# Eight of the last tile's projections computed in the attention stage, from operands read back from DRAM, and the layer norm's scaling moved from VectorE to ScalarE

## What is computed

```python
xn = layernorm(x)                      # x: (4, 1024, 512), no scale, no shift
q, k, v = xn @ Wq.T, xn @ Wk.T, xn @ Wv.T          # 16 heads of 32
scores = q @ k.T / sqrt(32), causal;   probs = softmax(scores)
attn = (probs @ v) @ Wo.T
gate = silu((xn @ fp8(gate_w)) * gate_scale)       # inner width 1536
up = (xn @ fp8(up_w)) * up_scale
ffn = ((gate * up) @ fp8(down_w)) * down_scale
out = x + attn + ffn
```

## Time and profile before

| what | value |
|---|---|
| runs | 1288.33, 1288.65, 1291.38 us, median 1288.65 |
| profiled execution, first to last instruction | 1287.4 us |
| PE busy | 1230.8 us, 96% |
| DVE, ACT, POOL busy | 1036.1, 895.2, 873.5 us |
| first stage | to 287.6 us |
| an iteration without and with output projections | 59.2 to 62.1, 59.7 us |
| transfers | 196 MB, mean 152 GB/s |

### The profile page before, as it was taken

The page is one execution under the profiler, slowest core; times in us unless marked ns, Lnnn a source line. Parts: engine busy times, 40 slices in busy tenths (PEclk is TensorE's granted clock), DMA queues, the critical chain, the costliest instruction groups (busy, mean ns, idle before and its releaser), DMA issues.

```text
span 1287.4 us, 32439 instructions
## 1 busy us (share of the span) xinstructions
PE 1230.8 (96%) x11756; PEld 822.8 (64%) x11756; DVE 1036.1 (80%) x2615; ACT 895.2 (70%) x1527; POOL 873.5 (68%) x1017
## 2 busy tenths in 40 slices
PE   4999999997999999999999999999999999999988
PEld 3444444445766767676777677777767677777663
DVE  8888887877877888788878788888888888878762
ACT  4322323228878888788888788888878888888770
POOL 1333232107877787788888888978878788888882
PEclk9999999998999999999999999999999999999999
DMA  8599998855645475666667676767686766767655
GB/s 271 161 250 243 256 258 232 203 152 120 135 96 129 96 151 99 145 114 148 127 138 153 127 153 125 157 104 166 115 158 114 160 121 137 143 128 165 105 113 121
DMA packets 427599, 196.07 MB, mean 152 GB/s; under 512 B 339248, under 2 KB 396592, under 8 KB 427440
## 3 DMA queue, kind: packets, MB, share of 16 engines
q1 hardware_dynamic: 409024, 177.22, 63.2%
q10 hardware_dynamic: 18416, 16.78, 4.9%
HBM read 72.89 MB, written 42.21 MB: 89 GB/s over the span
## 4 chain that ended last, share of the span: by engine, by line
PE 40%; POOL 16%; ACT 8%; issue 6%; DVE 5%; DMA 2%; SPq 0%; ACTq 0%; POOLq 0%; DVEq 0%
PE bank L1519 12%; PE bank L1533 12%; POOL row L1216 7%; PE bank L1495 6%; PE pair L210 3%; PE pair L1457 3%; POOL fuse L1198 3%; POOL probs L1064 3%; ACT probs L1263 3%; PE pair L1471 2%; POOL p L1210 2%; DMA p_t<-row 2%; ACT row L1287 2%; PE pair L1541 2%; DVE row_top L1399 2%
## 5 line engine op out<-in xcount | busy, mean ns | idle before, releaser
L1273 ACT ACTIVATE p<-pair,s_exp 128x512 f32<-128x512 f32 (+1 forms) x384 | 243.4, 634 | 143.3 <-PE pair L1457 142.0
L1216 POOL TENSOR_TENSOR row<-row 128x896 f16<-128x896 f32 (+1 forms) x128 | 256.2, 2011 | 7.7 <-ACT row L1287 7.7
L1263 ACT CAST probs<-p 128x512 f16<-128x512 f32 (+1 forms) x384 | 214.9, 560 | 15.1 <-POOL p L1210 12.6
L1064 POOL TENSOR_TENSOR probs<-p,probs 128x512 f16<-128x512 f32 x192 | 221.1, 1155 | 0.2
L1519 PE MATMUL bank<-shared,wu 128*128 128x256 f16 x1536 | 202.7, 276 | 0.0
L1519 PE MATMUL bank<-shared,wg 128*128 128x256 f16 x1536 | 202.5, 275 | 0.0
L1533 PE MATMUL bank<-wd,fuse 128*128 128x512 f16 x768 | 191.7, 380 | 0.8 <-DVE ff_out L1380 0.8
L1399 DVE TENSOR_REDUCE row_top<-pair 128x1 f32<-128x896 f32 (+1 forms) x128 | 147.5, 1152 | 35.4 <-PE pair L1475 34.9
L1210 POOL TENSOR_SCALAR_AFFINE_SELECT p<-p 128x128 f32<-128x128 f32 (+1 forms) x256 | 109.6, 433 | 93.2 <-ACT p L1273 91.3
L1198 POOL TENSOR_TENSOR fuse<-fu,fuse 128x512 f16<-128x512 f32 x96 | 118.5, 1235 | 65.3 <-ACT fuse L1302 65.1
L1519 PEld LDWEIGHTS bank<-shared,wg 128*128 128x128 f16 x1536 | 143.2, 98 | 25.0 <-DMA shared<-xn_parts 0.8
(11 more groups left out here) (155 smaller groups left out, 2106.0 us busy)
## 6 DMA issues: line engine op xcount, KB each, us to landing
q_st<-q_parts SPq DMA_DIRECT2D x192, 64.0 KB, 2.3
k_st<-k_parts SPq DMA_DIRECT2D x192, 64.0 KB, 2.0
v_parts<-res SPq DMA_DIRECT2D x8, 1056.0 KB, 6.8
v_sb<-v_parts SPq DMA_DIRECT2D x64, 132.0 KB, 2.2
xn_parts<-x_t SPq DMA_DIRECT2D x16, 512.0 KB, 8.8
q_parts<-qk_st SPq DMA_DIRECT2D x32, 256.0 KB, 5.5
k_parts<-qk_st SPq DMA_DIRECT2D x32, 256.0 KB, 4.2
shared<-xn_parts SPq DMA_DIRECT2D x16, 512.0 KB, 4.9
```

The lines of the kernel that those rows point to most:

```text
L1064: ops.tensor_tensor(probs[n % 2][:, LO, at], p32[e % RING][:, 0:UNIT_WIDTH[u]], probs[n % 2][:, HI, at], ALU.subtract).then_inc(signal, 1)
L1216: nc.gpsimd.tensor_tensor(row16[r][:, w:2 * w], row32[r][:, :], row16[r][:, 0:w], ALU.subtract).then_inc(row_lo, 1)
L1263: nc.scalar.copy(probs[n % 2][:, HI, u * 512:u * 512 + w], p32[e % RING][:, 0:w]).then_inc(p_hi, 1)
L1273: nc.scalar.activation(p32[e % RING][:, 0:w], st_bank[u % 2][:, 0:w], ACT.Exp, scale=s_exp[:, :]).then_inc(exp_done, 1)
```

## The change

Three things are done together.

1. Of the last tile (t = 7, `LAST`) only the four v projections stay in the first stage (`chunks`). In tile 6 the order is q, v, k (`chunk`). SP also stores the turned Wq and Wk to DRAM (`keep_weights`, 1 MB each, behind projections 7 and 8 of tile 6). In the second stage ACT loads the last tile's turned x (two halves of 0.5 MB) and Wq ahead of its first exponential, and Wk in head 1 of iteration 0. The eight q and k projections are made in the bank and at the steps of the output projections, in (iteration, head) (0, 1), (0, 2), (0, 3), (1, 2), (1, 3), (2, 2), (2, 3) and (3, 2), each in three pieces of 8 matmuls of 256 columns. ACT copies the HI part and DVE subtracts the LO part at step 4, SP stores it between the two turns of the rows, and PE waits for the LO part before the next turn of the maxima.
2. The normalisation of tiles 1 to 7 is made by ACT, as four activations (scale 1/sigma, shift -mean/sigma, both from POOL, which has two more links and a wait), behind projection 0 (6 in tile 0) and with `x_high` one projection later.
3. The plan of the feed-forward parts is denser: 4 parts in tiles 1, 2 and 6 and the last in tile 7; the row maxima of heads 0 and 1 move from tiles 6 and 7 to 5 and 6; the turn of head 0's maxima stands behind projection 1 of tile 6 and not 0.

```diff
+FF_STEPS = {2: ((1, 1), (1, 2), (1, 3)), 3: ((1, 3), (1, 4), (1, 5)), 4: ((1, 6), (1, 7), (1, 8)),
...
+            19: ((6, 0), (6, 1), (6, 1)), 20: ((6, 2), (6, 3), (6, 4)), 21: ((6, 5), (6, 6), (6, 7)),
+            22: ((6, 8), (6, 9), (6, 10)),
+            23: ((7, 9), (7, 10), (7, 11))}
+MAXIMA_AT, SPREAD_AT, FACTORS_AT = (6, 11), (7, 8), (7, 9)
+WEIGHTS_KEPT = {(6, 7): 0, (6, 8): 1}
...
+NORMALISED = (6, 0)
+LAST = NT - 1
...
+DEFERRED_AT = {(0, 1): 0, (0, 2): 1, (0, 3): 2, (1, 2): 3, (1, 3): 4, (2, 2): 5, (2, 3): 6, (3, 2): 7}
+DEF_STEP = {1: 0, 2: 1, 3: 2}
+DEF_SPLIT_STEP = 4
...
+        def chunks(t):
+            return range(12) if t < LAST else range(8, 12)
...
+        def chunk(t, c):
+
+            return (c, c + 4, c - 4)[c // 4] if t == LAST - 1 else c
...
+            def keep_weights(m):
+                sp.wait_ge(wt_act, 2 * (m + 1))
+                sp.wait_ge(wt_dve, 2 * (m + 1))
+                sp.dma_start(keep["w_dram"][m:m + 1].rearrange("a p w k d -> p (a w k) d"),
+                             w_t[m][:, :, :, :].rearrange("p w k d -> p (w k) d")).then_inc(w_stored, 16)
...
+            def normalise(t):
+
+                wait(act, xhi_done, t)
+                wait(act, xlo_done, t)
+                act.wait_ge(factor_link, FACTOR_LINKS * (t + 1))
+                for i in range(NB):
+                    last = nc.scalar.activation(xn[:, i, :], x_in[:, i, :], ACT.Identity, bias=shift[:, i:i + 1],
+                                                scale=rstd[:, i:i + 1])
+                last.then_inc(xn_done, 1)
...
-                    if c == (7 if t == 0 else 2) and has_next(t):
+                    if c == NORMALISED[t > 0] and has_next(t):
+                        normalise(t + 1)
+                    if c == NORMALISED[t > 0] + 1 and has_next(t):
                         x_high(t + 1)
...
-            last_tile = {0: ("magnitude 21", "add 21"), 1: ("off 21",), 2: ("magnitude 22",), 3: ("add 22",),
-                         4: ("off 22", "maxima"), 5: ("magnitude 23", "add 23"), 6: ("off 23",), 9: ("factors",)}
...
-                        if head == 1 and c == 0:
+                        if head == 1 and c == 1:
                             turn_maxima(nc, pe, rows, bank[7], ident, 0)
...
+            for half in range(2):
+                act.dma_start(late_x[half].rearrange("p w k t -> p (w k) t"),
+                              xn_dram[ds(NIT - 2 + half, 1)].rearrange("a p w k t -> p (a w k) t")
+                              ).then_inc(late_x_loaded[half], 16)
+            load_deferred_weights(0)
...
+            def high_of_deferred(d):
+                act.wait_ge(def_mm, d + 1)
+
+                wait(act, def_stored[d % 2], 16 * (d // 2))
+                nc.scalar.copy(def_st[d % 2][:, HI, :], misc[:, :]).then_inc(def_hi, 1)
...
+            def project_deferred(d, piece):
+
+                if piece == 0:
+                    pe.wait_ge(late_w_loaded[d // 4], 16)
+                    for half in range(2):
+                        pe.wait_ge(late_x_loaded[half], 16)
+                terms = [(wp, xp, kc) for wp, xp in X_TERMS for kc in range(KC)]
+                products = [(half, m) for half in range(2) for m in range(len(terms))]
+                for half, m in products[piece * 8:piece * 8 + 8]:
+                    wp, xp, kc = terms[m]
+                    mm = nc.tensor.matmul(misc[:, half * FT:(half + 1) * FT],
+                                          late_w[d // 4][:, wp, kc, d % 4 * P:(d % 4 + 1) * P],
+                                          late_x[half][:, xp, kc, :], start=(m == 0), stop=(m == len(terms) - 1))
...
+                            elif (it, s) in DEFERRED_AT:
+                                pe.wait_ge(def_lo, DEFERRED_AT[it, s] + 1)
```

More of the change, by code:

```diff
@@ L421, in tile @@
                                  ).then_inc(xt_stored, 16)
-                for c in range(8):
+                for c in chunks(t):
                     if (t, c) in HEADS_LOADED:
@@ new lines, in plan_of @@
+            def plan_of(t):
+                if t == 0:
+                    return first_tile
+                others = {(2, 11): ("max 3",), (3, 5): ("power 3",), (4, 11): ("low 3",),
+                          MAXIMA_AT: ("maxima",), FACTORS_AT: ("factors",)}
+                plan = part_steps(t)
+                for c in range(12):
+                    plan[c] = plan.get(c, ()) + others.get((t, c), ())
+                if t + 2 < NT:
+                    c = 9 if t + 2 == LAST else 10
+                    plan[c] = (f"statistics {t + 2}",) + plan[c]
+                return plan
```

199 lines of the change are left out of this document (129 added, 70 removed), and 6 rows, old and new, of the table FF_STEPS.

## The result

The changed kernel takes 1294.17 us (median of 4 runs, 1293.30 to 1295.46), the kernel before 1288.8 in the same runs: the ratio is 1.0040, 95% interval 1.0028 to 1.0053. Run once more later, beside an experiment, it took 1291.56 us, ratio 1.0018 (0.9999 to 1.0036). So it is slower by some 0.2 to 0.4% (the second time not clear of no change), and 21 to 23 us above the forecast of 1271. Its profiled execution spans 1291.6 us.

The account below looks back on a forecast made before the run. PE was taken to bound the first stage; the second had rests to fill. Terms -21.4 + 2.0 + 2.4 + 0.5 + 0.5 + 0.5 - 2.3 = -17.8 us took the 1287.4 span to 1269.6, plus 1.25: 1271 us, range 1265.5 to 1279.

Parts of the forecast that it names:

- Part 2: First stage, each tile: ACT normalises instead of DVE, covered by 3 us of slack; price 0, between 0 and 1 us per tile.
- Rival E: First stage, projections 1 and 2 of seven tiles: ACT's queue holds PE in each tile; 1292 us, chance 0.04.
- Part 1: First stage: eight projections leave, 20.7 us of PE, plus 0.65 us of waiting for POOL; gain 21.4 us.
- Part 3: Tile 6, denser DVE plan: PE waits behind projection 2 for the copied row of maxima, 2.0 us (0 to 3).
- Part 4: End of first stage: DVE's last "off" ends later, 2.4 us (1 to 4), plus 0.5 for the clock (0 to 1.7).
- Part 5: Start of second stage: ACT's three load issues cost 0.5 us (0 to 1.1), late operands 0.5 (0 to 2.4).
- rival B: Transfers bind: the first stage's stores only just fit and operands come 2.4 us late; 1275.5 us, chance 0.15.
- Part 6: Iterations 0 to 3 of the second stage: deferred projections fill PE's rests and lift its clock; -2.3 us (-5 to +5).

Follow-up runs that it names:

- e13: The changed kernel with DVE normalising tiles 1 to 7 again and POOL's two extra links gone: 1274.69 us.
- e2: The changed kernel with the up-weight loads of parts 13 and 16 issued at projection 8 of tiles 3 and 4, behind both x transposes: 1282.35 us.
- e1: The kernel before with only ACT's normalisation of tiles 1 to 7 and POOL's two extra links added: 1292.99 us, ratio 1.0044.
- e11: e8 with DVE normalising tiles 1 to 7 again, without POOL's two links or the edit on tile 0's wait: 1268.52 us.
- e3: The changed kernel with all twelve projections kept in tile 7, none deferred, and no late loads: 1308.08 us.
- e5: The changed kernel with ACT's first three late loads issued behind its second exponential of iteration 0: 1291.90 us.
- e6: The changed kernel with SP storing the fourth head's deferred projection (iterations 0 to 2) behind the row's second transpose: 1289.60 us.
- e8: e7 plus the edits of e5 and e6, and tile 0's normalisation not waiting for POOL's two new links: 1273.91 us.
- e7: The changed kernel with the edits of e2 and e4 together: 1276.29 us.
- e9: The changed kernel with the up-weight loads of parts 13 and 16 set to projection 5 of tiles 3 and 4, one later: 1290.56 us.
- e14: e11 with 14 instead of 7 matmuls keeping PE busy behind its last projection: 1268.60 us.
- e4: The changed kernel with DVE copying head 0's row of maxima ahead of its plan step behind projection 1 of tile 6: 1287.39 us.
- e15: The changed kernel with the up-weight loads of parts 13 and 16 set to projection 6 of tiles 3 and 4: 1288.89 us.
- e16: The changed kernel with ACT normalising tiles 2 to 7 behind its copy of projection 1 instead of 0: 1277.01 us.
- e19: e16 plus four edits of e8: row copy first, late loads later, store behind the row's transpose, tile 0 without the link wait: 1271.21 us.
- e10: e8 with 14 instead of 7 matmuls keeping PE busy behind its last projection: 1273.76 us.
- e12: e10 with DVE taking the row maxima ahead of its plan steps in tiles 5 and 6: 1273.55 us.

## Why the prediction was wrong

**The step that failed is Part 2**, "Price 0, between 0 and 1 us per tile". Undone, that one part gives 1274.69 (e13): inside the predicted range, 3.7 us above the forecast. All the rest was worth 14.6 us of the 17.8 forecast. Part 2 cost 17 to 20, of which the collision of one load and two transposes is the larger share (10.7 us in the profiles, tiles 3 and 4; moving the load alone, e2, brings the second stage 10.9 us forward). Three things were wrong in it.

First, it measured ACT's lateness by one user alone, PE's banks. There the slack of 3 us was nearly right: PE waits once at projection 5, the sign that was named for E, for 0.61 us in tile 2. It also saw that DVE would idle 3 us more and set that against DVE's spare time. But the same copies release DVE's low parts, these SP's stores, and SP's transposes are queued behind them. Second, it took the factors as ready 5.6 us behind the tile's start and 0.6 for two more links, from a kernel where ACT did not wait. In tile 3 of the changed kernel they are ready 8.2 behind it, 2.6 later than in tile 3 of before. Of these, 1.3 are DVE's lateness: its statistics of the next x begin 0.15 us behind the start of tile 3 (at 125.07), where in before and in e13 (at 120.89) they begin 1.2 ahead of it. The other 1.3 are POOL's longer chain, 8.1 us from there to the last factor instead of 6.8; one of the two new links took 0.85 us, not 0.20. Late copies make DVE late, late statistics make the factors late, and ACT waits for these again: that the price feeds itself so is read from the profile, no run isolated it. Third, at 18.2 us behind the tile's start the HI transpose falls 0.8 us ahead of the up load, with the cost measured by e2. With the old plan the load comes 2.6 to 3.0 us behind the transpose, HI lands in 9.7 and 10.1 us, and the part costs 5 us (e1); with the new plan 17 to 20. That the activations took 0.80 each, four in 2.93 instead of the 2.4 that I took, is the smallest piece. The estimate from the Trainium skill's budget (ScalarE: Activation LUTs, Rules for kernel authors), 0.73 us each and 2.9 for four, agrees with the 2.93 measured. The Trainium skill's rule there, to use VectorE for plain arithmetic, which it gives for the time per element, agrees with e13 and e11, though what cost most here was ACT's wait and not the activations. I had weighed it and found it covered by slack.

**Rival E** named ACT's queue and, at 1292, almost the time, with a chance of 0.04. But its path was another one: it needed activations 5.5 us longer, and PE held at its banks. Its chance was cut on that path, by the table load of the earlier trace rows, which held true. Nothing in it saw the wait at the head of the queue.

**Part 1.** 20.7 us by count; e3 against the changed kernel shows 18.8 at the start of the second stage. Counted from the start of tile 7 (272.9 in e3, 274.3 in the changed kernel) it is 20.2, so the count was nearly right; the other 1.4 us arise in the tiles ahead, where both kernels have the same work and e3 waited 7.8 us for x before tile 4 instead of 8.9.

**Part 3.** The wait was foreseen in its place and for its cause; 2.0 forecast, 3.85 measured with ACT late and 2.44 without (e13). With ACT late, DVE's low part of projection 1 ends 8.5 us behind the tile's start instead of the 7.1 reckoned, and "off" then takes 1.79 us instead of 0.95. Missed was the clock behind the wait, 1.7 us, and that the same denser plan makes PE wait in tile 5 for the maxima's banks and the last turn: 0.91, 0.48, 0.38 and 1.11 us, 2.9 together (2.4 in e13).

**Part 4.** 2.4 forecast; from the end of the last projection to the first scores it takes 3.58 instead of 2.53 us, 1.05 more. DVE's "off" is the last work, as said (287.77 to 288.72).

**Part 5.** The issues: 0.5 forecast; they fill 2.8 us, and from the first scores to the turn of the maxima it takes 11.5 us for 9.0. I took each at the 0.36 us of the earlier trace rows; 0.34, 1.26 and 1.18 was the truth. The operands land at 302.0 and are used at 306.0 without a wait, so the 0.5 for them was not needed, and rival B isn't there. How much of the 2.5 us is the issues and how much the low clock, e5 does not settle.

**Part 6.** -2.3 forecast, +1.2 measured (241.5 against 240.3), and -1.6 to -3.0 with SP's store behind the second transpose of the row (seven profiles, e6 -1.7, e8 -2.8, e11 -3.0). Iterations 1 and 2 took the 59.7 to 60 and the full clock of the forecast once the transpose was in time. Iteration 3 kept its full clock in most profiles, but in five (e2, e7, e9, e13, e14) it has a stretch at 0.50 and takes 60.8 to 61.0 us. The sentence that fell is "which is due later anyway": it was due 2.4 us earlier than it landed, in the fourth head of iteration 0.

## What to carry to other kernels

Before work is moved to an idle engine, ask what its queue holds while it waits: an instruction with 3 us of waiting and 3 of work delays everything behind it by 6, and the price is to be followed through every user of the delayed results (here DVE, SP's stores, SP's transposes), not only to the engine that bounds the stage. If it must stand there, put it behind what others wait for: one projection later took away half of the waiting, load and transpose changed their order, and 14 to 17 us came back. When a queue slips by a few us, check which transfers of other queues it now meets.

## What the runs showed of the hardware

- A load of 384 KB issued from ACT 0.8 us behind an x transpose of SP: in tiles 3 and 4 of eight profiles (the changed kernel twice, e3, e4, e5, e6, and tile 3 of e9 and e15) HI took 9.3 to 16.2 us to land. With the load 0.4 to 1.6 us ahead of it (e13, e16, e19) it took 7.7 to 9.3, with the load 2.2 to 4.8 behind (tile 4 of e9 and e15) 5.3 to 7.3, with none within 6 behind (e2, e7, e8, e10, e11, e12, e14) 5.1 to 8.0. Between these lie the kernel before and e1, with a gate load 2.6 to 3.0 behind: 8.7 to 10.1. While it lasts the DMA engines show the same share of busy time and move a third of the bytes (80 and 252 GB/s from 148 to 156 us). It isn't the distance alone: in tile 1 of the changed kernel a down load 0.8 us behind HI left it at 6.4 us and a gate load 0.4 behind LO left that at 6.8. And behind LO of tile 3 an up load 0.4 to 1.6 us later (e2, e7, e8, e10, e11, e12, e14) left it at 7.7 to 9.9 us. What makes the difference for HI in tiles 3 and 4 is open.
- Issuing a load took ACT 0.34, 1.26 and 1.18 us for three in a row at the start of the second stage, and one transpose held SP for 10.56 us (3.8 in the same tile of before).
- The clock fell to 0.50 during PE's wait of 7.03 us and 0.4 us behind that of 3.85 us. It isn't certain to: in e15 the same wait was 3.82 us long, the clock stayed at 1.00, and the 12 matmuls behind it took 2.75 us. At the sparse start of the second stage it fell in every profile, for about 3 to 10 us whatever the pause ahead of it (0.6 to 2.1 us).
